# Routing table of layer 1 built by one-hot products, shared expert beside the routing, join between VectorE's copies, rows finished in one step

## The reference

```python
# layer 0: x -> layernorm -> h
x  = x + ssd(h)                                    # 32 heads, a gated recurrence over the tokens
y  = moe0(h)     # 16 experts of width 128, 4 of them per token (2 groups of 4 allowed); gates normalised
sh = (silu(h @ w1_s.T) * (h @ w3_s.T)) @ w2_s.T    # a shared expert, width 256, for every token
x  = x + y + sh
# layer 1: x -> layernorm -> h
q, k, v = (sigmoid(4 * (batchnorm(h @ W.T) - 1)) for W in (Wq, Wk, Wv))   # statistics over all tokens
x  = x + attention of 16 heads without softmax, out = q @ (k.T @ v) * scale @ Wp.T + bp
x  = x + moe1(h)  # 8 experts of width 512, 2 of them per token
```

## Time and profile before

| | us |
|---|---|
| median of 3 runs | 2511.88 (2510.11 to 2513.68) |
| the profiled execution, whole | 2510.14 |
| its span in the trace | 2508.4 |
| TensorE busy | 2187.4 (87%) |
| VectorE busy | 1566.1 (62%) |
| GpSimd busy | 1450.4 (58%) |
| ScalarE busy | 1197.7 (48%) |
| mean granted TensorE clock | 0.947 |

### The profile page before, as it was taken

One profiled execution on the slowest core, in us unless ns is written; L12 is line 12 of the kernel. 1 busy time (PEld: TensorE's weight loads), 2 busy tenths in 40 slices (PEclk: granted clock), 3 DMA queues, 4 the chain that ended last, 5 costly groups with the idle time before them and its releaser, 6 DMA issues. The chain is left out here.

```text
span 2508.4 us, 40252 instructions
## 1 busy us (share of the span) xinstructions
PE 2187.4 (87%) x12164; PEld 1578.4 (63%) x12164; DVE 1566.1 (62%) x3353; ACT 1197.7 (48%) x2681; POOL 1450.4 (58%) x1257
## 2 busy tenths in 40 slices
PE   4774899999999999999999988999187279999997
PEld 2442677777777777777777766666143265666664
DVE  4086888888888888888888845666575152222221
ACT  2233677777777777777777722222133141111111
POOL 0332577777777777777777755556633503444443
PEclk9986999999999999999999999999689599999999
DMA  6634444544544544544545457664540027222221
GB/s 243 257 129 116 118 140 137 147 147 141 157 138 140 151 140 143 157 136 143 152 136 144 127 171 226 209 198 127 191 151 1 1 94 222 47 46 43 43 46 19
DMA packets 206733, 330.63 MB, mean 132 GB/s; under 512 B 60224, under 2 KB 148672, under 8 KB 206272
## 3 DMA queue, kind: packets, MB, share of 16 engines
q1 hardware_dynamic: 148080, 233.65, 31.5%
q0 software_dynamic: 28928, 53.75, 8.5%
q10 hardware_dynamic: 29520, 40.66, 5.1%
HBM read 240.83 MB, written 88.04 MB: 131 GB/s over the span
## 5 line engine op out<-in xcount | busy, mean ns | idle before, releaser
L1046 DVE SCALAR_TENSOR_TENSOR m_cv<-m_hp,conv,m_cv 128x256 f32<-128x256 f32 x864 | 416.8, 482 | 112.2 <-ACT m_cv L945 91.0
L1443 PE MATMUL e_u<-wup,e_xgT 128*128 x1152 | 422.8, 500 | 17.2 <-DVE e_xgT L1397 13.4
L1381 ACT ACTIVATE e_sil<-e_u 128x128 f32<-128x128 f32 (+1 forms) x216 | 83.0, 384 | 573.1 <-PE e_u L1443 512.7
L1134 PE MATMUL m_hp<-xnT,wpj 128*128 128x259 f32 x1152 | 306.4, 389 | 28.4 <-PEq L144 25.7
L872 POOL TENSOR_TENSOR m_er<-m_er,m_cT 128x1024 f32<-128x1024 f32 x128 | 302.0, 2359 | 46.8 <-DVE m_ar L1053 46.8
L983 ACT ACTIVATE m_ar<-m_ar,m_ta 128x128 f32<-128x128 f32 x1024 | 318.8, 391 | 0.8
L1443 PEld LDWEIGHTS e_u<-wup,e_xgT 128*128 128x128 f32 x1152 | 203.7, 192 | 149.8 <-issue 138.7
L1142 PE MATMUL m_gp<-xnT,wpj 128*128 128x256 f32 x1024 | 268.6, 384 | 11.2 <-ACT m_gT L963 11.2
L1134 PEld LDWEIGHTS m_hp<-xnT,wpj 128*128 128x128 f32 x1152 | 215.5, 193 | 90.4 <-issue 49.0
L1340 POOL DMA_INDIRECT out<-e_y,e_tab x72 | 112.8, 1567 | 231.2 <-DVE e_y L1410 190.9
L879 POOL TENSOR_TENSOR m_hdd<-m_hdt,m_tb 128x512 f32<-128x512 f32 x128 | 131.0, 1043 | 193.8 <-DVE m_hdt L1061 193.8
(11 more groups left out here) (307 smaller groups left out, 3934.3 us busy)
## 6 DMA issues: line engine op xcount, KB each, us to landing
m_ar<-acum_rows_dram SPq DMA_DIRECT2D x512, 128.0 KB
m_er<-eacum_rows_dram SPq DMA_DIRECT2D x128, 512.0 KB
rows_by_slot<-blank_rows ACTq DMA_DIRECT2D x1, 18576.0 KB, 59.5
e_xg<-rows_by_slot ACTq DMA_DIRECT2D x132, 129.0 KB
m_xrow<-xn_rows SPq DMA_DIRECT2D x32, 512.0 KB, 5.2
b_work<-y_rows SPq DMA_DIRECT2D x16, 1024.0 KB, 7.8
wup<-in_w SPq DMA_DIRECT2D x8, 1024.0 KB
wpj<-in_w_proj SPq DMA_DIRECT2D x1, 4352.0 KB, 18.1
```

What stands on the lines that cost most here:

```text
L1046: v_.scalar_tensor_tensor(o, hp[n % 2][:, j:j + BLK], conv[:, c, j:j + 1], o, ALU.mult, ALU.add).then_inc(tapped.sem, 1)
L1134: ins = mm(hp[n % 2][:, 0:PW], w_proj[:, kd, col:col + P], xpad[:, kd, ds(i * BLK, PW)], start=kd == 0, stop=kd == KD - 1)
L1443: ins = nc.tensor.matmul(u_ps[a.slot(2)][b][:, 0:width], xgT[:, a.slot(2), c, :], wup[:, c, ds(e * (2 * f) + b * width, width)], start=c = ...
```

## The change

1. **One `Shared`**, for all 8 groups (16 ups), in `route_phase` only. The two halves of an up have semaphores of their own (`s_up1`, `s_up3`, `s_silu`, `s_kept`), the output has two buffers, and the bias add is no longer there. `Join.add_bias` does it on POOL, 8 times, in the loop of layer 0's experts.
2. **`norm_phase`** has no shared expert and does not wait for its stores; the row stores are waited for by SP at the end of `route_phase`. POOL makes `u` and `z` of the step sizes, group by group. Seven small weights are loaded ahead of the shared expert's.
3. **`route_phase`**: ScalarE does the exponentials first, VectorE starts with `middle_of_vector` (with the denominator, once POOL's) and then does the routing; the sums stand ahead of up 8 and the counting behind up 13 in TensorE's list. `etab` is made on 128 partitions, 2 columns, and goes to one partition through DRAM in `ssd_phase`.
4. **`Join`**: one operation in a tile, between `e_xgT` and `e_hid`, in 8 of 11 tiles from tile 54; the loads of groups 0 and 1 stand ahead of the layer-1 weights.
5. **`bridge_phase`**: `b_rstd` and `b_xn` are made in the step of their group. The table of layer 1 is a sum of 64 products in TensorE's bank 0, one for each tile of tokens and choice: POOL makes `pick` (one-hot of the slot within a tile, 128x128), VectorE `load` (one-hot of the tile, once times the token and once times the gate, 2 of 128x72), in a ring of 12, spread over the last 12 units of `AFTER`. Four operations then make `source`, `aimed` and `gate` in SBUF. The scatters, the padding and the table in DRAM go. `etab` is made behind the routing and goes through DRAM.
6. **`expert_phase` of layer 1** takes these lists; it loads no table.

```diff
@@ class Shared
     def up(self, pe, j):
-        if j:
-            pe.wait_ge(self.s_kept, j)
-        for bank, off in ((self.h1, 0), (self.h3, FS)):
+        g, c = divmod(j, 2)
+        for bank, off, done, kept in ((self.h1, 0, self.s_up1, self.s_silu), (self.h3, FS, self.s_up3, self.s_kept)):
+            if j:
+                pe.wait_ge(kept, j)
...
-    def add_bias(self, pool, i):
-        pool.wait_ge(self.s_dk, 2 * i + 2)
-        self.nc.gpsimd.tensor_tensor(self.out[:], self.out[:], middle(self.b_out[:], BIG), ALU.add).then_inc(self.s_b, 1)
...
@@ norm_phase
+                for g in range(NG):
+                    at = slice(g * BIG, (g + 1) * BIG)
+                    pool.wait_ge(s_qc, g + 1)
+                    link(v.tensor_tensor(u[:, at, :], small[:, at, E0:SM0], middle(bias_dt[:, 0, :], BIG), ALU.add))
+                    link(v.tensor_scalar(z[:, at, :], u[:, at, :], 0.0, 2.0, ALU.max, ALU.mult))
+                    link(v.tensor_tensor(z[:, at, :], u[:, at, :], z[:, at, :], ALU.subtract))
...
@@ decay_work
+    SUMS, COUNT = 8, 14
...
         for j in range(UPS):
-            if j == EARLY:
-                side.down(pe, EARLY // 2 - 1)
+            if j == SUMS:
                 pe.wait_ge(s_adt, 1)
...
             side.up(pe, j)
-            if j % 2 == 0 and j and j != EARLY:
+            if j % 2 == 0 and j:
                 side.down(pe, j // 2 - 1)
+            if j == COUNT - 1:
+                pe.wait_ge(s_rowc, 2)
+                count()
...
@@ class Join
+    FIRST = 54
+
+    def add_bias(self, pool, n):
+        g, rest = divmod(n - self.FIRST + 4, 11)
+        if rest or not 0 <= g < NG:
+            return
+        pool.wait_ge(self.s_in[g % 2], (g // 2 + 1) * 48)
+        self.nc.gpsimd.tensor_tensor(self.sr[:, g % 2], self.sr[:, g % 2], middle(self.b_out[:], BIG), ALU.add).then_inc(self.s_b, 1)
+
     def tile(self, dve, n):
-        t, rest = divmod(n - 40, 3)
-        if rest or not 0 <= t < T:
+        g, at = divmod(n - self.FIRST, 11)
+        if not (0 <= g < NG and at < 2 * BIG):
             return
...
@@ bridge_phase, VectorE's rows
-                    a = s.back(1)
-                    if a.inside(NG):
-                        at = slice(a.n * BIG, (a.n + 1) * BIG)
-                        reached(dve, s_std0, a)
+                        reached(dve, s_std0, s)
                         v.reciprocal(rstd[:, at], tmp[:, at]).then_inc(s_rstd, 1)
...
@@ bridge_phase, the table: GpSimd, VectorE, TensorE
-                pool.wait_ge(s_zeroed, 16)
                 pool.wait_ge(s_rt, 1)
-                scatter_slots(pool, posi, pay, table, range(T), k_n, s_scat)
-                pool.wait_ge(s_scat, T * k_n * 16)
+                pool.wait_ge(s_turn, 3)
+                for n in range(ENTRIES):
+                    t, q = divmod(n, k_n)
+                    if n >= RA:
+                        pool.wait_ge(s_tab, n - RA + 1)
+                    g_.tensor_scalar(pick[:, n % RA, :], slot_row[:], slot_f[:, t, q:q + 1], None, ALU.is_equal).then_inc(s_pick, 1)
...
                 for n in AFTER:
+                    for m in entries(n):
+                        t, q = divmod(m, k_n)
+                        if m >= RA:
+                            dve.wait_ge(s_tab, m - RA + 1)
+                        for a, val in enumerate((token_f[:, t:t + 1], gates[:, t, q:q + 1])):
+                            ins = v.tensor_scalar(load[:, m % RA, a, :], slot_row[:, 0:nt], tile_f[:, t, q:q + 1], val,
+                                                  ALU.is_equal, ALU.mult)
+                        ins.then_inc(s_load, 1)
                     unit(n)
...
+                    for m in entries(n):
+                        pe.wait_ge(s_pick, m + 1)
+                        pe.wait_ge(s_load, m + 1)
+                        mm(table[:, 0:2 * nt], pick[:, m % RA, :], load[:, m % RA].rearrange("p a j -> p (a j)"),
+                           start=m == 0, stop=m == ENTRIES - 1).then_inc(s_tab, 1)
```

More of the change, by code:

```diff
@@ L251, in store @@
-    def store(self, sp, i):
-        sp.wait_ge(self.s_b, i + 1)
-        sp.dma_start(tokens(self.sh_dram, self.groups[i] * BIG, BIG), self.out[:]).then_inc(self.s_st, 16)
+    def store(self, sp, g):
+        sp.wait_ge(self.s_dk, 2 * g + 2)
+        sp.dma_start(tokens(self.sh_dram, g * BIG, BIG), self.out[:, g % 2]).then_inc(self.s_st[g % 2], 16)
     def stored(self, sp):
-        sp.wait_ge(self.s_st, len(self.groups) * 16)
-def norm_phase(nc, sem, tag, k, xs, x_dram, xnT, rows, w_small, small, ns, loads, blank, shared, s_shared_w):
+        for n in range(2):
+            sp.wait_ge(self.s_st[n], NG // 2 * 16)
@@ L263, in norm_phase @@
+def norm_phase(nc, sem, tag, k, xs, x_dram, xnT, rows, w_small, small, ns, loads, blank, xn, s_row, bias_dt, u, z, s_weights):
     ctx = ExitStack()
@@ L294, in step @@
                         sp.dma_start(tokens(rows, g.n * BIG, BIG), xn[:, g.slot(4)]).then_inc(s_row[g.slot(4)], 16)
-                    j = s.n - 7
-                    if j >= 0 and j % 2 == 0 and j // 2 < len(side.groups) - 1:
-                        side.store(sp, j // 2)
-                pipeline(NG, 4, step)
-                side.store(sp, len(side.groups) - 1)
-                for r in range(4):
-                    sp.wait_ge(s_row[r], NG // 4 * 16)
-                side.stored(sp)
+                pipeline(NG, 1, step)
             @block.vector
@@ L346, in _ @@
             def _(pool):
-                for j in range(UPS):
-                    side.multiply(pool, j)
-                    if j % 2 == 0 and j:
-                        side.add_bias(pool, j // 2 - 1)
-                side.add_bias(pool, len(side.groups) - 1)
+                v = nc.gpsimd
+                link = Chain(pool, s_u)
+                pool.wait_ge(s_weights, 16 * N_LOADS)
+                link(v.tensor_tensor(bias_dt[:, 0, :], bias_dt[:, 0, :], bias_dt[:, 1, :], ALU.add))
+                for g in range(NG):
[4 more added lines that the diff above has]
+                    link(v.tensor_tensor(z[:, at, :], u[:, at, :], z[:, at, :], ALU.subtract))
             @block.scalar
@@ L494, in _ @@
                 sp.wait_ge(s_blank, 16)
+                for r in range(4):
+                    sp.wait_ge(s_row[r], NG // 4 * 16)
             @block.vector
@@ L700, in sync @@
                          far[:, :, 0:b * VW].to_broadcast([P, HQ, b * VW])).then_inc(s_st, 16)
-        for i in range(UPS // 2 - 2):
-            side.store(sp, i)
+        for g in range(3):
+            side.store(sp, g)
         for sm in s_big:
@@ L1247, in expert_loads, with expert_phase @@
     return load
-def expert_phase(nc, sem, tag, k, rows, table, by_slot, etab, wup, wdown, e_n, f, nt, y_dram, load, s_first=None, beside=None):
+def expert_phase(nc, sem, tag, k, rows, lists, by_slot, etab, wup, wdown, e_n, f, nt, y_dram, load, s_first=None, beside=None):
     ctx = ExitStack()
@@ L1312, in _ @@
                     load(sp, n, s_w)
-                    if n == 0:
-                        for t in range(U, nt, U):
-                            sp.dma_start(tab[:, t:t + U, :], entries[:, t:t + U, :]).then_inc(s_rest, 16)
                 sp.wait_ge(s_w, 32 * e_n)
@@ L2047, in program @@
             with Semaphores(nc, sem) as own:
[L2048 removed]
+                expert_phase(nc, own, "e1_", k, rows, lists1, None, etab1, wup, wdn, E1, F1, NT1, out, load, s_first=s_out)
 def layout(i):
```

371 lines of the change are left out of this document (179 added, 192 removed).

## The result

The changed kernel takes 2404.93 us (median of 4 runs, 2403.37 to 2406.89) where the kernel before takes 2510.99 (2505.12 to 2513.68) beside it: a ratio of 0.9585, 95% interval 0.9571 to 0.9599. That is 106 us less. The forecast was 2383, 129 less, with a range of 2350 to 2424.

A forecast was written before the change was run, and what follows sets the result against it. The recurrence and second expert loop keep TensorE busy nearly throughout, and the change does not enter their loops; elsewhere the terms -49 + 0 - 26 - 16 - 33 - 5 = -129 take 2511.9 to 2383 us, range 2350 to 2424.

The forecast's parts named there:

- Norm stage: First stage: without its half of the shared expert the next stage starts at 73, not 122.07: -49 us.
- Routing stage: Layer 0's routing: the four shared-expert groups moved in fill TensorE's gaps, about 106 us against 107: 0.
- Rival (a): Shared work is moved, not saved, lengthening the routing stage: +20 to +43 us, 2403 to 2426; chance .09.
- First expert loop: Layer 0's experts: cheaper joins -21, first join's wait -9, bias add +4, in all -26 us (-10 to -32).
- The 4 us for the bias: First expert loop: cost taken for GpSimd's eight bias adds, between 0 if hidden and 19 in the open.
- Bridge, rows: Bridge before the units: finishing rows in their loading step, no table filling or transfer: -16 us (-3 to -24).
- one step out of the pipeline: -12: Bridge rows: finishing a group's rows in the step that loads it saves one step of 12.0 us.
- Table: Bridge, table and v steps: one-hot products replace 64 scatters and the waits beside them: -33 us (-45 to -17).
- T0 + 67: Bridge: forecast end of VectorE's table loads, 67 us after the units that follow the rows start.
- rival b: GpSimd and VectorE exclude each other: +16 us for the table, +15 for the bias, 2414; chance .10.
- Rival (c): Bridge: the v steps' stalls aren't the scatters', so the 48.7 us stay: 2432; chance .06.
- Rival (d): Bridge table: ring loads and picks wait out each other, 3 us an entry, slower than before: 2544; chance .03.

The follow-up runs named there:

- kind B: Chips where the kernel before takes 2457 to 2459 us; there the unchanged changed kernel took 2395.75 us, ratio 0.9751.
- experiment 1: Changed kernel with the stores of the shared expert's groups 0 to 2 placed between the three decay-table fills: 2390.40 us, ratio 0.9724.
- experiment 4: Changed kernel with VectorE again finishing a group's rows (reciprocal and xn) one step later in the bridge: 2407.18 us, ratio 0.9796.
- the controls: Both kernels rerun unchanged: the changed one took 2406.61 us, ratio 0.9583, on kind A and 2395.75 us, ratio 0.9751, on kind B.
- kind A: Chips where the kernel before takes about 2512 us, as in the first result; there the unchanged changed kernel took 2406.61 us, ratio 0.9583.
- Experiment 2: Changed kernel with the table loads of the next unit ahead of a unit's statistics in VectorE's bridge list: 2390.76 us, ratio 0.9729.
- experiment 7: Changed kernel with 64 indirect scatters, into a table nothing reads, put back on GpSimd behind its last pick: 2478.88 us against 2406.61.
- the pieces: Changed kernel with the output bias added in four operations of 128x256 a group instead of one of 128x1024: 2398.15 us, ratio 0.9760.

## Why the prediction was right, and where it was off

The direction, the range and the order of the terms held; the sum was 23 us too good, and several terms came out near by errors that cancelled. That it was this near is also luck of the chip: on kind B the same change gives 63 us, less than half of the 129. Point by point:

- **Norm stage**: forecast 73, measured 68. Two misreadings cancelled in part. The first four groups took 18.3 us (TensorE's transposes of the first start at 22.10, those of the fifth at 40.44), where 4 x 7.2 was put: the 6.8 of the earlier trace rows has projections in it, which the first two groups do not have behind them yet (their transposes stand 3.14 apart). And the projections that run on behind the last transposes (54.03 to 63.85) were not put down. The transposes of the first three groups take 1.97 us, those of the later ones about 1.09, the prices that the forecast took for the low and the high clock, although the view by stretch gives a granted clock of 1.00 from 22 to 34 us.
- **Routing stage**: the step that failed is what the stage waits for. What I left out is the stores' place in SyncE's list, behind the fills, which now come right behind the weights' loads: 11 us. TensorE's work was put 6 us too long. Without the wait (experiment 1) the counting comes 77.6 us after the stage's start (67.06 to 144.69), where the forecast has 156.6 - 73 = 83.6; half of that is a misreading of the earlier trace rows, where 3.60 is the length of a row of eight matmuls, while such rows start 3.44 apart (120.61 to 127.48 for two), 3 us over 20 of them. So that the counting came at 156.9 (forecast 156.6) and the recurrence's first operation at 179.4 (near 180) was luck: a start 5 us earlier, work 6 us shorter, a wait of 11. Experiment 1 gives the stage as 100: the term should have been -7 for the work and +11 for the wait. Rival (a) did not come: TensorE's gaps took the moved work.
- **First expert loop**: the mechanism held. The joins in the gap are nearly free (in experiment 4, on kind B, elevens of joined tiles took 19.7 to 20.0 us and unjoined ones 19.2 to 19.8), and the 8.8 us at the first join went. Forecast -26, measured -17.8, and -22.3 in the controls on kind A. The 4 us for the bias was mis-sized on kind A (about 9) and too large on kind B (1.2), where the stage's -31.5 is at the good end, -32. The rest of what is missing in the first profile is open.
- **Bridge, rows**: forecast -16, measured -6.9. The step that failed is "one step out of the pipeline: -12". It takes out a step at the end, 7.3 us, by experiment 4. The -4 for the filling and for less work in front was worth nothing that a run shows. The root's round trip was covered, as said (0.35).
- **Table**: the step that failed is the price of a load, 0.17 from a 128x4 operation. On 72 columns it is 0.23 alone, 7.7 us more over 128, and up to 0.35 beside a pick, another 4.1; that is 33.6 - 21.8 = 11.8, all of the 12 us by which the end missed T0 + 67, since the waits of 8.6 are about what I had put down for blocking (67 - 59, 8). Experiment 2 gives 7 of them back. The v steps were right, and so, on kind A, was the reason that their stalls would go.
- **The port pair (rival b)**: present but small. The excess of a load beside a pick is 0.12 us in 34 steps, not a pick's length; that makes 4 us in all, not 16. The Trainium skill (page "SBUF — State Buffer", section "SBUF: two separate sides") states that the pair is an exclusive lock, held for the whole instruction. By that rule a load could stand for up to the 0.60 of a pick; this trace does not agree, since in the changed kernel no load is longer than 0.45 and the loads go on beside picks that follow each other without a gap. In the rows of before it fits (2.26 beside 2.33). Of the other half of rival (b), 15 us for the bias, some 9 came on kind A and 1.2 on kind B; no run shows whether the port has a part in the 9.
- **Rival (c)**: the stalls of the v steps are the scatters' on kind A (experiment 7), and on kind B the same scatters make none. So my -33 rested on a wait that one kind of chip has and the other has not. What the scatters take from the other engines there is not settled: the crawl of single matmuls, 2.1 and 2.8 us apart in turn, with no semaphore named, looks like engines that are not fed with instructions, but no run here shows that.
- **Rival (d)**, the table slower than what it replaces, came true on kind B as a term (+34 us), with an entry at 0.77 us (49.5 us for 64), far from 2.5; it does not turn the whole, since norm stage and first loop give 87 us there.

Open: why kind A and kind B differ beside the scatters, and why one e_hid comes late behind a whole bias addition on A alone (the pieces were never run there by themselves); and whether on kind B the kernel with the old scatters and all else changed is faster than any here. By the stages it would be: 2396 less 34 is about 2362, or 2371 if the 9 us that the rest of the bridge and the last loop gained there went back too, an estimate that was not run.

## What to carry to other kernels

A stage saved at the end of a pipeline is worth a step of the drain, not a step of the loop: read the pace where it falls away. When buffers are freed by stores, follow the store into its issuing queue: a transfer with many short rows in front of it can hold the queue (15.5 and 12.1 us here). And where a gain rests on a wait that no row explains, measure the kernel before on a second chip ahead of building on it.

## What the runs showed of the hardware that I had not expected

- The same program took 2457 to 2459 us on two chips and 2509 to 2512 on another and in the first result, with one stretch of 56 us as the whole difference: 64 indirect scatters of 12 bytes a partition, 1.0 to 1.1 us each on both, stop TensorE, ScalarE and VectorE for up to 19 us at a time on the one kind (52.9 us in experiment 7) and not at all on the other.
- Two fills of short rows (1024 of 256 and of 384 bytes), issued from 71 on behind the loads of the big weights, held SyncE for 27.6 us; issued at 95 and 109 they took 5.1 together. The fill of blank rows was under way in both cases (until 116 or 117), so it alone does not hold them; the loads of the big weights had landed by 91 in the second case and at 93 in the first. Whether these loads or the fills before in the queue held them is open.
- A one-hot entry of a 128x144 table cost 0.39 us on TensorE (25.2 us busy for 64), 0.59 on GpSimd (37.6) and 0.53 on VectorE (33.6). TensorE had been idle for 6.7 us in front of the first of them, and the matmuls behind that gap took up to twice their time (2.88 for ten, then 1.39).
